# Expert stage of a vision layer: second layer one group behind, products of one tile shape together, two output tiles

## What is computed

```python
xf = layernorm(h).reshape(-1, 64)
logits = xf @ router_w.T + router_b          # 32 experts
idx = argmax(logits, axis=-1)                # one expert for each token
hid = relu(einsum('nd,ndh->nh', xf, W1[idx]) + b1[idx])      # 16 hidden
out = relu(einsum('nh,nhd->nd', hid, W2[idx]) + b2[idx])
h = h + out
```

## Time and profile before

| | |
|---|---|
| median of 3 runs | 618.31 us (617.52 to 618.47) |
| the profiled execution | 618.27 us, span 616.5 us |
| PE busy | 552.0 us, 90% |
| DVE busy | 490.0 us, 79% |
| ACT busy | 408.8 us, 66% |
| POOL busy | 350.1 us, 57% |
| expert stage | from 395.8 us to the end, 220.7 us |
| split products L1703 | 1024 passes, mean 393 ns |
| second layer L1776 | 512 passes, mean 382 ns |
| relus of ACT L1788 | 96, 58.9 us, mean 684 ns |
| chain that ended last | PE psum L1703 10%, L1776 9%, L1761 3%, L1695 3% of the span |

### The profile page before, as it was taken

The page is one execution under the profiler, slowest core; times in us unless marked ns, Lnnn a source line. Parts: engine busy times, 40 slices in busy tenths (PEclk is TensorE's granted clock), DMA queues, the critical chain, the costliest instruction groups (busy, mean ns, idle before and its releaser), DMA issues. The chain is left out here.

```text
span 616.5 us, 18701 instructions
## 1 busy us (share of the span) xinstructions
PE 552.0 (90%) x7273; PEld 394.3 (64%) x7274; DVE 490.0 (79%) x879; ACT 408.8 (66%) x723; POOL 350.1 (57%) x388
## 2 busy tenths in 40 slices
PE   5897999999999999999656776499999999999995
PEld 4796789999898899897212222355555555555552
DVE  4798788888888888886799999677777777777762
ACT  2475788888888888888697576135555555555543
POOL 8303367778779887774898698542333423334220
PEclk9999899999999999999779788879999999999998
DMA  9622222222222222210000000001011010110101
GB/s 193 107 41 46 59 62 57 59 59 57 63 59 54 59 58 61 62 35 3 1 0 0 0 1 2 3 3 26 18 24 22 21 25 19 23 22 21 26 19 27
DMA packets 62381, 23.05 MB, mean 37 GB/s; under 512 B 45780, under 2 KB 62292, under 8 KB 62292
## 3 DMA queue, kind: packets, MB, share of 16 engines
q1 hardware_dynamic: 61472, 21.69, 17.2%
q10 hardware_dynamic: 692, 0.13, 0.1%
q0 software_dynamic: 128, 0.00, 0.0%
HBM read 5.02 MB, written 4.19 MB: 15 GB/s over the span
## 5 line engine op out<-in xcount | busy, mean ns | idle before, releaser
L762 DVE TENSOR_REDUCE work<-psum 128x16 f32<-128x1024 f32 x64 | 78.0, 1218 | 31.2 <-PE psum L597 31.2
L697 ACT ACTIVATE work<-work 128x1024 f32<-128x1024 f32 x64 | 67.8, 1060 | 23.5 <-DVE work L767 23.2
L1788 ACT ACTIVATE hid<-psum,b1c 128x512 f32<-128x512 f32 x96 | 58.9, 684 | 32.2 <-PE psum L1695 32.2
L767 DVE TENSOR_TENSOR work<-psum,work 128x1024 f32<-128x1024 f32 x64 | 78.3, 1224 | 2.2
L1678 POOL TENSOR_TENSOR m_sq<-m_xc 128x256 f32<-128x256 f32 x32 | 19.6, 613 | 100.1 <-DVE m_xc L1839 100.0
L705 ACT ACTIVATE work<-psum 128x512 f32<-128x512 f32 x128 | 70.7, 618 | 2.4 <-PE psum L612 1.5
L612 PE MATMUL psum<-kc,work 128*128 128x128 f32 x512 | 67.7, 275 | 4.2 <-ACT work L697 3.5
L1703 PE MATMUL psum<-x_t,w1x 64*64 64x256 f32 x1024 | 70.9, 393 | 0.0
L628 PEld LDWEIGHTS psum<-work 128*64 128x64 f32 x2048 | 62.3, 138 | 5.3 <-issue 5.3
L628 PE MATMUL psum<-work 128*64 128x18 f32 x2048 | 65.5, 212 | 0.0
L612 PEld LDWEIGHTS psum<-kc,work 128*128 128x128 f32 x512 | 58.8, 141 | 8.7 <-ACT work L697 4.4
(11 more groups left out here) (197 smaller groups left out, 1291.4 us busy)
## 6 DMA issues: line engine op xcount, KB each, us to landing
work<-big_bc SPq DMA_DIRECT2D x256, 32.0 KB, 2.0
h_all<-in_x SPq DMA_DIRECT2D x16, 256.0 KB, 5.3
work<-big_a SPq DMA_DIRECT2D x32, 128.0 KB, 2.2
out<-out_st SPq DMA_DIRECT2D x128, 32.0 KB
w1x<-in_L_ffn_W SPq DMA_DIRECT2D x2, 128.0 KB, 4.1
kc<-constants SPq DMA_DIRECT2D x1, 202.0 KB, 2.7
w2x<-in_L_ffn_W SPq DMA_DIRECT2D x1, 128.0 KB, 4.1
work<-in_L_tok_qkv_w ACTq DMA_DIRECT2D x2, 32.0 KB, 2.5
```

Source lines behind the costliest of these rows:

```text
L697: act.activation(prob[:, f], prob[:, f], ACT.Exp).then_inc(prob_done, 1)
L762: dve.tensor_reduce(top[:, f, :].rearrange("p (g h) -> p g h", g=4), sc, AX.X, ALU.max).then_inc(top_done, 1)
L767: dve.tensor_tensor(prob[:, f].rearrange("p (g h) k -> p g h k", g=4), sc, top[:, f, :].rearrange("p (g h) -> p g h", g=4).unsqueeze(3).br ...
L1788: act.activation(hid[:, g, :], psum[:, HID_BANK[g], :], ACT.Relu, bias=b1c[:, g:g + 1]).then_inc(relu_act, 1)
```

## The change

The steps now run from i = -2 to QUADS + 3. On every engine the work is put at other lags and in another order:
- PE: x transposes (quad i - 1), y transposes (i + 1), choice transposes (i - 2), router products (i - 1), output transposes (i - 4), all eight split parts (i - 2) in one row, masks (i - 2), bias and second layer (i - 3). Inside the split parts PE waits for `x_half` before parts 4 and 6, until parts 0 and 1, then 2 and 3, have ended.
- `mark_t` and `hid` are doubled, as the second layer reads those of the quad before; relus no longer wait for it at once.
- ACT: x copy, o copy (i - 4), choice copy, y stage (i + 2), relus.
- DVE: h, sum and `m_xc` (i + 1), output (i - 4), choice (i - 1), relu (i - 2), square sum and variance (i + 1). For i below 3 the choice comes first.
- Two output tiles with a semaphore each; SP's loop is written out; of the last quad's four stores two are issued by ACT.

```diff
-    mark_t = sb("mark_t", [96, 2, 2 * P], BF16)
-    hid = sb("hid", [P, 4, 4 * P])
+    mark_t = sb("mark_t", [96, 2, 2, 2 * P], BF16)
+    hid = sb("hid", [P, 2, 4, 4 * P])
...
-    out_st = sb("out_st", [P, 4, C])
+    out_st = sb("out_st", [P, 2, 4, C])
...
-    LAST = QUADS + 2
...
+    LAST = QUADS + 3
...
-for i in range(LAST + 1):
+for i in range(-2, LAST + 1):
...
-    with sp.Fori(0, QUADS) as i:
+    for i in range(QUADS):
         sp.wait_ge(out_made, i + 1)
-        store_quad(sp, out, out_st[:, :, :], i, stored)
...
+        store_quad(sp, out, out_st[:, i % 2], i, stored[i % 2], (0, 1) if i == QUADS - 1 else (0, 1, 2, 3))
...
+    for par in range(2):
+        sp.wait_ge(stored[par], QUADS // 2 * 64)
...
-        if live(i, 0):
...
+        if live(i, 1):
...
+            pe.wait_ge(xh_done, i)
...
+        if live(i, -1):
+            pe.wait_ge(y_staged, i + 2)
+            if not first(i, -1):
+                pe.wait_ge(h_done, i + 1)
+            if live(i, 5):
+                pe.wait_ge(out_made, i - 4)
...
         if live(i, 2):
-            pe.wait_ge(x_copied, i - 1)
-            for g, b in X_PARTS[:4]:
-                x_part(i - 2, g, b, True)
...
             pe.wait_ge(chosen, i - 1)
...
             for s in range(4):
-                if s == 3:
-                    pe.wait_ge(x_half, i * 16 - 24)
                 m = pe.matmul(psum[0:96, 2, s % 2 * 256 + s // 2 * P:s % 2 * 256 + s // 2 * P + P],
...
-        if live(i, 3):
-            pe.wait_ge(o_copied, i - 2)
-            pe.wait_ge(h_done, min(i + 1, QUADS))
...
-        if live(i, 2):
-            for g, b in X_PARTS[4:]:
-                x_part(i - 2, g, b, False)
...
         if live(i, 1):
             pe.wait_ge(x_copied, i)
...
+        if live(i, 4):
+            pe.wait_ge(o_copied, i - 3)
+            pe.wait_ge(h_done, min(i + 2, QUADS))
+            if not first(i, 4):
+                pe.wait_ge(out_made, i - 4)
+            for n in range(2):
+                m = pe.transpose(psum[:, 0, 256 + n * P:256 + n * P + P], o_t[:, n, :], ident)
...
         if live(i, 2):
             if not first(i, 2):
-                pe.wait_ge(o_copied, i - 2)
+                pe.wait_ge(relu_act, i * 3 - 6)
+                pe.wait_ge(relu_dve, i - 2)
+            for n, (g, b) in enumerate(X_PARTS):
+                if n in (4, 6):
+                    pe.wait_ge(x_half, i * 16 - 32 + (n - 2) * 2)
+                x_part(i - 2, g, b, n < 4)
+            if first(i, 2):
+                pe.wait_ge(masks_set, 2)
+            pe.wait_ge(mark_copied, i - 1)
+            for g in range(4):
+                mask(i - 2, g)
+        if live(i, 3):
+            pe.wait_ge(relu_act, i * 3 - 6)
+            pe.wait_ge(relu_dve, i - 2)
+            if not first(i, 3):
...
             for b in range(2):
-                pe.matmul(psum[64 * b:64 * b + 64, 6, 0:256], b2p[:, :], mark_t[:, b, :],
+                pe.matmul(psum[64 * b:64 * b + 64, 6, 0:256], b2p[:, :], mark_t[:, (i - 3) % 2, b, :],
...
+            for g in range(4):
...
+        if live(i, 4):
+            act.wait_ge(o_done, i * 2 - 6)
+            if not first(i, 4):
+                act.wait_ge(o_turned, i - 4)
+            act.activation(o_t[:, :, :].rearrange("p k t -> p (k t)"), psum[:, 6, 0:256], ACT.Copy
+                           ).then_inc(o_copied, 1)
...
+        if live(i, -2):
+            if i >= -1:
+                act.wait_ge(y_turned, i + 2)
+            stage_y(i + 2)
...
             relu(i, 0)
             relu(i, 1)
             relu(i, 3)
...
+    act.wait_ge(out_made, QUADS)
+    store_quad(act, out, out_st[:, (QUADS - 1) % 2], QUADS - 1, stored[(QUADS - 1) % 2], (2, 3))
...
+        if live(i, 1) and i < 3:
+            choose(i)
...
+            if not first(i, -1):
+                dve.wait_ge(xh_done, i + 1)
             dve.scalar_tensor_tensor(xc[:, :, :], nsum[:, :].unsqueeze(2).broadcast_to([P, 4, C]),
...
+        if live(i, 4):
+            dve.wait_ge(o_turned, i - 3)
...
+            if not first(i, 5):
+                dve.wait_ge(stored[i % 2], (i - 4) // 2 * 64)
+            dve.scalar_tensor_tensor(out_st[:, i % 2], psum[:, 0, 256:512].rearrange("p (s d) -> p s d", s=4),
...
+        if live(i, 1) and i >= 3:
+            choose(i)
+        if live(i, 2):
+            dve.wait_ge(hid_done, i * 4 - 5)
...
+                dve.wait_ge(o_done, i * 2 - 6)
+            dve.tensor_scalar(hid[:, i % 2, 2, :], psum[:, HID_BANK[2], :], b1c[:, 2:3], 0.0, ALU.add, ALU.max
+                              ).then_inc(relu_dve, 1)
...
+        if live(i, -1):
+            dve.wait_ge(sq_done, i + 2)
             dve.tensor_reduce(ssum[:, :], sq[:, :, :], AX.X, ALU.add).then_inc(ssum_done, 1)
-            dve.wait_ge(ssum_done, i + 1)
+            dve.wait_ge(ssum_done, i + 2)
             dve.tensor_scalar(var[:, :], ssum[:, :], 1.0 / C, LN_EPS, ALU.mult, ALU.add
                               ).then_inc(var_done, 1)
```

More of the change, by code:

```diff
@@ L1571, in backwards, with store_quad @@
     return bass.AP(tensor=ap.tensor, offset=ap.offset, ap=[list(ap.ap[0]), [-1, n]])
-def store_quad(eng, out, src, i, done):
+def store_quad(eng, out, src, i, done, parts=(0, 1, 2, 3)):
     at = i // 2 * 512 + i % 2 * 32 + i // 16 * L
     flat = out.rearrange("b t d -> (b t) d")
[L1578 to L1583, removed]
+    for n in parts:
+        k, b2 = n // 2, n % 2
+        a = flat[bass.ds(at + (k * 16 + b2 * L), 1), :]
+        dst = bass.AP(tensor=a.tensor, offset=a.offset, ap=[[SIDE * C, 8], [C, 16], [1, C]],
+                      dep_tracking_offset=a.dep_tracking_offset)
+        eng.dma_start(dst, src[:, 2 * k + b2, :]).then_inc(done, 16)
 def experts(nc, ctx, t, out):
@@ L1636, in experts @@
     o_done, o_copied, o_turned = sem("m_o_done"), sem("m_o_copied"), sem("m_o_turned")
[L1637 to L1642 removed]
+    out_made, stored = sem("out_made"), (sem("stored0"), sem("stored1"))
+    LAST = QUADS + 3
     HID_BANK = (4, 5, 7, 3)
@@ L1749, in body @@
                     m.then_inc(x_turned, 1)
+                if live(i, -1):
[5 more added lines that the diff above has]
+                    for n in range(2):
+                        m = pe.transpose(psum[:, 0, n * P:n * P + P], y_st[:, n, :], ident)
+                    m.then_inc(y_turned, 1)
                 if live(i, 2):
-                    for g, b in X_PARTS[4:]:
-                        x_part(i - 2, g, b, False)
                     if first(i, 2):
[L1754 to L1757, removed]
+                        pe.wait_ge(masks_set, 1)
+                    pe.wait_ge(chosen, i - 1)
+                    if not first(i, 2):
+                        pe.wait_ge(mark_copied, i - 2)
+                    for s in range(4):
+                        m = pe.matmul(psum[0:96, 2, s % 2 * 256 + s // 2 * P:s % 2 * 256 + s // 2 * P + P],
+                                      mark[:, s, :, :].rearrange("p j e -> p (j e)"), ident_b[:, :],
+                                      start=True, stop=True, skip_group_check=True)
+                    m.then_inc(mark_turned, 1)
                 if live(i, 1):
@@ L1763, in body @@
                     m.then_inc(logits_done, 1)
+                if live(i, 4):
[3 more added lines that the diff above has]
+                        pe.wait_ge(out_made, i - 4)
+                    for n in range(2):
+                        m = pe.transpose(psum[:, 0, 256 + n * P:256 + n * P + P], o_t[:, n, :], ident)
+                    m.then_inc(o_turned, 1)
                 if live(i, 2):
@@ L1769, in body @@
                                   start=True, stop=False, skip_group_check=True)
[L1770 to L1774, removed]
+                    for g in range(4):
                         for b in range(2):
                             m = pe.matmul(psum[64 * b:64 * b + 64, 6, 0:256], w2x[:, g, :],
-                                          hid[:, g, 256 * b:256 * b + 256], start=False, stop=(g == 3),
+                                          hid[:, (i - 3) % 2, g, 256 * b:256 * b + 256], start=False, stop=(g == 3),
@@ L1787, in relu @@
                 act.wait_ge(hid_done, i * 4 + (g - 7))
-                act.activation(hid[:, g, :], psum[:, HID_BANK[g], :], ACT.Relu, bias=b1c[:, g:g + 1]
+                act.activation(hid[:, i % 2, g, :], psum[:, HID_BANK[g], :], ACT.Relu, bias=b1c[:, g:g + 1]
                                ).then_inc(relu_act, 1)
@@ L1808, in body @@
                                    ).then_inc(x_copied, 1)
-                if live(i, 2):
-                    if not first(i, 2):
-                        act.wait_ge(o_done, i * 2 - 4)
+                if live(i, 4):
[4 more added lines that the diff above has]
+                                   ).then_inc(o_copied, 1)
+                if live(i, 2):
+                    act.wait_ge(mark_turned, i - 1)
+                    act.activation(mark_t[:, i % 2, :, :].rearrange("p b q -> p (b q)"), psum[0:96, 2, :], ACT.Copy
```

(10 more changed lines are left out.)

106 lines of the change are left out of this document (32 added, 74 removed).

## The result

The changed kernel takes 612.0 us in the median (610.8 to 612.25), the kernel before 617.91 us beside it on the same chip: a ratio of 0.9901, 95% interval 0.9883 to 0.9918. The forecast was 611.0 us. The profiled execution took 612.22 us for a span of 610.5 us, 6.1 less than before (to two places the spans are 616.53 and 610.46).

| | before | forecast | after |
|---|---|---|---|
| start of the stage (first y copy of ACT) | 395.78 | 395.78 | 396.58 |
| to the first masks | 12.50 | 15.6 | 15.69 |
| first to second masks | 6.39 | 4.65 | 5.07 |
| 30 steps to the last masks | 191.4 | 183.1 | 182.3 |
| last masks to last output | 4.58 | 6.5 | 6.46 |

A forecast was written before the change was run, and what follows sets the result against it. PE bounds the step, with DVE and POOL nearly alike (6.12). Fill 411.4, 4.15 + 0.5, 30 steps of 6.13, -0.83, tail 6.5 + 0.42 and 3.2 give a 609.2 span; with 1.74 outside, 611.0 us (607.5 to 613, chance 0.50).

The forecast's parts named there:

- the router's new wait: On PE, router products wait for ACT's x copy and can start at 0.92, not at 0.72.
- The step of PE: PE's inner step: 6.13 us from x to next x, against 6.41 before.
- Rival 1: Full gain: router doesn't wait or hand-over takes half, and POOL's ring is shorter; 5.87 a step, 603.2 us; chance 0.12.
- Rival 3: Slower: PE empties at each of two waits between split products; 0.44 a step, 6.57, 624 us; chance 0.12.
- First masks: Fill: first masks at 411.4 instead of 408.28, low clock lasting until about 410.6; cost 3.1 us, bounds 1.3 to 3.6.
- The step before the last: Tail: x, y and router groups are gone, so split products start at 0.9 instead of 1.73: -0.83.
- The ring of DVE and POOL: Loop from centred x through DVE's operations and POOL's two back to the next: 6.12 a step, bounds 6.04 to 6.28.
- rival 2: DVE and POOL's loop is the longer: 6.28 a step, 615.5 us, PE waiting for h at output transposes; chance 0.19.
- First to second masks: Fill: 6.13 - 1.98 = 4.15 without a second layer, plus 0.5 once for DVE's late h at the first output transposes.
- From last output to end: Stores at the end: 5.4 before, 3.2 left, after 0.42 for the output itself.
- two now go to ACT's queue, 1.68 less: Last quad's stores: two of SP's four issues, 0.84 apart, move to ACT, saving 1.68.
- four issue gaps instead of seven: PE's step: idle weight-load gaps at changes of tile shape fall from seven to four, each change costing 0.15 us.

The follow-up runs named there:

- the freed router: Changed kernel with output transposes ahead of the router products, in their own columns of bank 6, and ACT's o copy ahead of its x copy: 605.71 us, ratio 0.9819.
- the three together: Changed kernel with output transposes ahead of the router, variance ahead of DVE's relu, and quad 0's first half early in the fill: 606.14 us, ratio 0.9821.
- the early half alone: Changed kernel with quad 0's first half of split products behind its router products, step 2's y transposes behind the router: 610.55 us, ratio 0.9897.

## Why the prediction was right, step by step

The median of 612.0 us lies 1.0 above the forecast. The mechanism was right too: three changes of shape fewer, the router's new wait, and a step that PE alone sets. Some terms of the sum were mis-sized.

**Confirmed as worked out.** The step of PE: router load at 0.92 after x (481.78 - 480.86 = 0.92), output at 1.40 (1.42), split at 1.73 (1.73), masks at 3.62 (3.62), bias 4.15 (4.15), next x 6.11 (6.13). Four "issue" gaps. Rival 1's condition, 5.87 once nothing waits, is the 5.88 of the freed router. Rival 3's alternative, that each wait for the first half exposes itself, did not come about; the waiting load came at 483.42 - 482.59 = 0.83, as worked out, and shows an idle 0.19 that costs nothing. First masks 15.69 after the start of the stage against 15.6, with the low clock to 411.6 (410.6). The step before the last was 0.77 shorter (0.83). The last output came 6.46 after the last masks (6.5).

**The ring of DVE and POOL was mis-sized:** 6.12 (6.04 to 6.28) in the sum, 5.92 in the run. xc to output took 0.34 (0.40), output to choice 0.33 (0.37), relu to square sum 0.66 (0.74). I had taken the distances between starts from places where something else than the operation ahead held the next one, and the lower bound took only one of them down. So it did not bind beside PE's 6.13, and rival 2 had less behind it than its 0.19.

**First to second masks:** 4.65 in the sum, 5.07 in the run, and for another reason. The 4.15 still held the output transposes (0.22), which don't exist yet in this step, so the sum should have begun at 3.93. The 0.5 put down for DVE's h at the first output transposes did not occur. Instead the router of step 3 waited 1.18 for ACT's x copy (1.33 idle on its load), as ACT's three relus of quad 0 (412.69 to 414.53) stood ahead of the copy, where inside the row the copy comes when they are done. I had followed ACT's new order only for a full row.

**From last output to end:** 3.62 in the sum, 4.34 in the run. The term that failed is "two now go to ACT's queue, 1.68 less": it was worth 0.41. The first issue of ACT took 1.44 us and the second 0.65, 2.12 with what lies between them, a little more than three issues on SP (3 x 0.645 = 1.94). The written-out loop gave 1.07, above the 0.5 put down for it and above its bound of 0.7, as it shortened the start of the first issue too.

**Sum of the misses:** start of the stage and first masks +0.87 (0.80 of it outside the stage), second masks +0.42, 30 steps -0.74, tail -0.04, end +0.72: +1.2, the 610.5 against the 609.2 of the sum. Leaving out the 0.80 from ahead of the stage, 0.43 is left. That this is so little is luck in part: the 30 steps gave 0.74 more than summed, and second masks and end took 1.14 back.

**The sign "four issue gaps instead of seven"** was counted from the changes of shape and not from the rows. The kernel before shows six such gaps a step (0.39, 0.17, 0.39, 0.17, 0.39, 0.42), and none from router to bias, though that change costs time as well: the router group took 0.59 there and 482.27 - 481.78 = 0.49 where output transposes of its own shape follow.

## What to carry to other kernels

Count the changes of tile shape in an inner loop of short products and price them from two like groups, one with and one without a change; then look at each product that was moved forward for the copy it now waits for, since here that wait (6.103 - 5.880 = 0.22 a step) was as large as one and a half changes, and one more exchange of two groups took it away. A wait of PE for its own products costs nothing when it asks for products some passes back and 0.39 a step when it asks for the last. At the ends of a pipeline follow each queue's own order step by step: a gain in the fill was twice taken back, in most or in all, by the engine that was not yet done with the step before.

## What the runs showed of the hardware

The first DMA issue of the stage on ACT's queue took 1.44 us and the next 0.65 (1.45 and 0.65 in the kernel with the freed router), where SP's take 0.60 each. Why the first is long the traces don't show. On SP a store in the hardware loop takes 0.84 from issue to issue and in the written-out one 0.645. The granted clock can fall back in mid-stage: in the three together at 413.0, when PE had stood idle since 411.5. From 406.2 to 413.0 PE was busy for 3.65 us there, and for 4.54 in the kernel with the early half alone, whose stage starts within 0.1 us of it and where the clock stayed up. Between independent operations of DVE the next starts 0.08 to 0.09 before the one ahead ends (relu 0.74 long, the next start 0.66 later; xc 0.43, 0.34).
